# Bias rows on 128 partitions, an earlier end of a graph's preparation, and two neighbour rows scaled on GpSimd, in a graph network kernel

## The chip, the cores and the metric

The kernel runs on one core of a Trainium2 chip. The metric is the device time of the whole program in microseconds: 4361.47 us is the median of three runs before the change (4359.83 to 4365.68). The engines are named as the profile does: PE is TensorE (matmuls), PEld its weight loads, DVE is VectorE, ACT is ScalarE, POOL is GpSimd, SP is SyncE, which here only issues DMAs.

## The reference, cut to what matters

There are 32 graphs of 512 nodes with 128 features. The adjacency is sparse, about one entry in sixteen.

```python
# layer 0
adj  = adj + eye
dis  = adj.sum(axis=2) ** -0.5
x    = layernorm(x + dis[:, :, None] * adj * dis[:, None, :] @ (x @ W) + bias)
# layer 1, over all pairs i, j
m_j, m_i = x @ W1[:D], x @ W1[D:]
pre  = m_j[:, None, :, :] + m_i[:, :, None, :] + b1
msg  = gelu(layernorm(pre, g1, be1))             # exact gelu
agg  = einsum('bijo,bij->bio', msg, adj)
upd  = layernorm(concat([x, agg]) @ W2 + b2, g2, be2)
out  = layernorm(x + upd)
```

Only pairs with an edge count in `agg`, and the kernel works on those alone.

## The kernel before, in words

For each graph and each of its four tiles of 128 destination nodes the kernel lists the neighbours of every node. A slot (a *neighbour row*) takes one neighbour j on each of 128 partitions. A tile has 40 neighbour rows, cut into seven **units** of 6, 6, 6, 6, 6, 5 and 5 rows; a graph has 28 units (GC), the program 896. The rare tile with more neighbours goes through an overflow loop.

The layer norm of a pair is `r * (mj + mi) + be1` after its means are taken out of the weights. Its factor r is found for all pairs of a graph beforehand, as a reciprocal square root. For one unit c the work passes the engines in this order, a step apart each, and every engine runs its own list in order (`steps(cx, i)` is that list for step i):

- DVE in step c-1 makes `pick` (a one-hot matrix with r as its value), L998 and L993.
- PE in step c: two matmuls with a 3-row operand put the bias be1 into PSUM (`z_even_ps` or `z_odd_ps`, L1260), and five or six fp32 matmuls of `mi_g` with `pick` add to it (L1264). The three rows are be1 split into three bf16 parts, multiplied with three rows of ones.
- ACT in step c+1 copies r out of PSUM (L643) and scales the neighbour rows of the unit with it (`tmp`, L647), one instruction for each row.
- DVE in step c+2 adds `tmp` to PSUM (`msg`, L969 and L972) and makes `spread` from the adjacency (L1028, L1024).
- ACT in step c+3 applies the gelu (L634).
- PE in step c+4 adds the unit into `agg_even_ps` or `agg_odd_ps` (L1227).

There are two z buffers, two `tmp` buffers and four `msg` buffers. z of unit c waits for the DVE addition of unit c-2 (`c_z`).

Between these stand three side jobs. **Preparation** of the next graph but one part at a time: step i does part s = (i + 8) mod 28, by the numbers S_XT, S_DEG, ... at the top of the file. PE parts share the bank `p_ps`, in the order of the numbers F_XT, ... : each waits until the one before was copied out. The end of it, in order: h_g (S_H), its transpose (S_HT), miT, mjT (L1123), the norms of mj (S_NRM, L1135), four matmul pairs for the variances (S_V, L1146 and L1147), then on ACT in one part two copies, a table load, the reciprocal square root of 2048 columns (S_SEED, L578), and with the next gelu a second table load; then one correction of the root in four parts (S_ROOT, ACT L583 and L586, DVE L856 and L859), and four parts of four indirect DMAs each on POOL (S_SCATTER, L449), which write all of it by neighbour rank into a table in HBM. SP then reads the table back (`nbr`, `nbr_root`, `nbr_heavy`) when all 16 have landed, in `read`.

**Sorting** of the next tile: from step 3 of each seven, PE transposes `nbr` (T_EDGE, L1159) and `nbr_root` (L1165), and counts edges with triangular matrices (L1169, L1173, and four matmuls onto 32 partitions each, L1178). The first L1159 of a graph waits for the read-back of that graph's table. **Finishing** of the graph before: u (L1241 to L1243, the last of them with 3 rows of b2), statistics, scale, residual and the store.

POOL's list has, beside the scatter, the sums over `pre_g`, the edge mask (L417), powers of -1/2 (L391, L396, L463), the residual (L466, L469), `hb_g` (L432), copies of `mj_g` into `stage` (L425) and `rank_heavy` (L455).

## Time and profile before

| | |
|---|---|
| median of three runs | 4361.47 us |
| profiled execution, its own time | 4369.12 us |
| its span | 4367.4 us |
| mean granted clock | 0.96 of full |
| PE busy | 4004.6 us, 92% |
| ACT busy | 3479.5 us, 80% |
| DVE busy | 3154.2 us, 72% |
| POOL busy | 1499.9 us, 34% |
| first unit's bias matmul starts | 141.5 us |

A busy share is the time in which at least one instruction of the engine ran, by the record. An idle time before an instruction is put down to what came last. Where a row says "issue", the engine's own instruction stream brought the next one only then. The 28 units of a graph take about 129 to 134 us; the stretch from 2150 to 2280 us that is read below is one of them, from unit 0 to unit 27.

### The profile page before, as it was taken

What the parts mean: (1) busy time and instruction counts of PE and PEld (TensorE: products, weight loads), DVE (VectorE), ACT (ScalarE), POOL (GpSimd) and SP (SyncE); (2) the same over time, 40 slices, a digit from 0 to 9 for tenths busy, and PEclk for the clock granted to TensorE, in tenths of its full rate; (3) what the DMA queues carried; (4) which work ended last, traced back from release to release, by engine and by line L of the source; (5) the groups of instructions that cost most, each with busy time, mean ns of one, the idle gap of its engine ahead of it and who ended that gap; (6) DMA issues with size and microseconds to landing.
All of it is one profiled execution on the core that took longest, in us unless ns stands there. A gap on an engine that the chain in (4) does not pass through costs nothing.

```text
span 4367.4 us, 95715 instructions
## 1 busy us (share of the span) xinstructions
PE 4004.6 (92%) x30270; PEld 3283.8 (75%) x30399; DVE 3154.2 (72%) x6981; ACT 3479.5 (80%) x9481; POOL 1499.9 (34%) x1205
## 2 busy tenths in 40 slices
PE   3799999999989999999999999999999999999998
PEld 2677777777768777778777777777777777777776
DVE  3577777777767777767777768777777777768776
ACT  2687888878868878877887878888888888878887
POOL 2333432233413334323343233343233343223331
PEclk8899999999989999999999999999999999999999
DMA  1222221122202222112221112222122221112210
GB/s 42 72 70 78 70 73 38 57 79 78 71 24 64 79 70 78 44 52 72 78 71 65 41 61 78 79 70 68 37 62 79 78 71 62 46 59 78 66 58 15
DMA packets 245645, 276.71 MB, mean 63 GB/s; under 512 B 22320, under 2 KB 204080, under 8 KB 245040
## 3 DMA queue, kind: packets, MB, share of 16 engines
q1 hardware_dynamic: 212272, 168.62, 12.9%
q0 software_dynamic: 32768, 100.70, 6.2%
q8 instruction: 298, 4.88, 0.5%
q14 instruction: 307, 2.51, 0.2%
HBM read 160.17 MB, written 109.05 MB: 62 GB/s over the span
## 4 chain that ended last, share of the span: by engine, by line
PE 56%; ACT 12%; issue 11%; POOL 9%; DVE 5%; DMA 4%; SPq 2%; POOLq 0%; DVEq 0%; ACTq 0%; PEldq 0%
PE z_even_ps L1264 11%; POOL table L449 9%; PE agg_odd_ps L1227 9%; PE z_odd_ps L1264 8%; PE agg_even_ps L1227 7%; ACT tmp L647 4%; PE z_even_ps L1260 3%; PE z_odd_ps L1260 2%; DMA nbr_heavy<-table 2%; PE p_ps L1146 2%; PE p_ps L1147 2%; PE p_ps L1090 2%; DMA table<-stage,row_id 2%; ACT msg L634 2%; ACT root L578 1%
## 5 line engine op out<-in xcount | busy, mean ns | idle before, releaser
L647 ACT ACTIVATE tmp<-nbr,r_sb 128x128 f32<-128x128 f32 x4864 | 1519.3, 389 | 29.1
L998 DVE SCALAR_TENSOR_TENSOR pick<-rank,root_p 128x512 f32<-128x512 bf16 (+3 forms) x1664 | 895.5, 566 | 69.8 <-ACT rank L597 69.8
L1028 DVE SCALAR_TENSOR_TENSOR spread<-rankT,nbr 128x512 f32<-128x512 bf16 (+3 forms) x1664 | 918.7, 580 | 0.0
L449 POOL DMA_INDIRECT table<-stage,row_id x512 | 617.9, 1207 | 551.5 <-issue 504.9
L1264 PEld LDWEIGHTS z_even_ps<-mi_g,pick 128*128 128x128 f32 x5120 | 643.9, 201 | 152.2 <-issue 152.2
L634 ACT ACTIVATE msg<-msg 128x768 f32<-128x768 f32 (+1 forms) x896 | 727.7, 812 | 32.3 <-issue 29.2
L1264 PE MATMUL z_even_ps<-mi_g,pick 128*128 128x129 f32 x5120 | 733.0, 295 | 0.0
L1264 PEld LDWEIGHTS z_odd_ps<-mi_g,pick 128*128 128x128 f32 x5120 | 608.8, 192 | 144.8 <-issue 144.8
L1264 PE MATMUL z_odd_ps<-mi_g,pick 128*128 128x129 f32 x5120 | 694.9, 285 | 0.0
L1227 PE MATMUL agg_odd_ps<-spread,msg 128*128 128x128 f32 x5120 | 671.8, 282 | 21.4 <-DVE spread L1028 19.3
L1227 PEld LDWEIGHTS agg_odd_ps<-spread,msg 128*128 128x128 f32 x5120 | 636.0, 199 | 24.1 <-DVE spread L1028 23.5
L1227 PE MATMUL agg_even_ps<-spread,msg 128*128 128x128 f32 x5120 | 647.2, 276 | 0.0
L1227 PEld LDWEIGHTS agg_even_ps<-spread,msg 128*128 128x128 f32 x5120 | 610.6, 193 | 0.0
L972 DVE TENSOR_TENSOR msg<-z_odd_ps,tmp 128x768 f32<-128x768 f32 x320 | 305.1, 954 | 357.5 <-ACT tmp L647 356.5
L972 DVE TENSOR_TENSOR msg<-z_even_ps,tmp 128x768 f32<-128x768 f32 x320 | 305.1, 954 | 261.2 <-ACT tmp L647 257.8
L455 POOL TENSOR_TENSOR rank_heavy<-rank,behind 128x256 bf16<-128x256 bf16 x128 | 110.8, 865 | 746.2 <-ACT rank L597 745.5
L643 ACT COPY r_sb<-z_even_ps 128x6 f32<-128x6 f32 x448 | 71.1, 159 | 275.0 <-PE z_even_ps L1264 271.6
L425 POOL COPY stage<-mj_g 128x512 f32<-128x512 f32 x128 | 95.1, 784 | 556.0 <-ACT mj_g L557 556.0
L969 DVE TENSOR_TENSOR msg<-z_odd_ps,tmp 128x384 f32<-128x384 f32 (+1 forms) x256 | 112.7, 480 | 222.3 <-ACT tmp L647 220.3
L417 POOL TENSOR_SCALAR edge<-adj_g 128x512 bf16<-128x512 f32 x128 | 263.8, 2078 | 26.3 <-ACT edge L519 26.3
L1260 PE MATMUL z_even_ps<-be_split,ones 3*128 3x387 bf16 x896 | 231.4, 339 | 25.7 <-DVE msg L972 14.6
L1260 PE MATMUL z_odd_ps<-be_split,ones 3*128 3x387 bf16 x896 | 223.6, 329 | 12.1 <-DVE msg L972 1.5
(206 smaller groups left out, 5129.6 us busy)
## 6 DMA issues: line engine op xcount, KB each, us to landing
nbr<-table SPq DMA_DIRECT2D x128, 512.0 KB, 4.0
adj_g<-in_adj SPq DMA_DIRECT2D x32, 1024.0 KB, 5.5
nbr_root<-table SPq DMA_DIRECT2D x128, 256.0 KB, 4.7
nbr_heavy<-table SPq DMA_DIRECT2D x512, 32.0 KB, 3.6
x_g<-in_x SPq DMA_DIRECT2D x32, 256.0 KB, 2.9
table<-stage,row_id POOLq DMA_INDIRECT x512, 2.7
out<-out_sb SPq DMA_DIRECT2D x32, 256.0 KB, 2.3
w_sb<-in_L_gnn_W SPq DMA_DIRECT2D x2, 128.0 KB, 2.3
```

Of the source, the lines that this page charges most:

```text
L417: last = pool.tensor_scalar(edge[:, it, :], adj_g[:, it, :], 0.0, 0.0, ALU.is_equal, ALU.is_equal)
L449: pool.indirect_dma_start(table[q], bass.IndirectOffsetOnAxis(ap=row_id[:, jt * TB + it:jt * TB + it + 1], axis=0), stage[:, jt, it, :], N ...
L455: pool.tensor_tensor(rank_heavy[:, at(k), :, :], rank[:, at(k), 0:HEAVY_W].unsqueeze(1).to_broadcast([P, HEAVY_TILES * HEAVY_T, HEAVY_W]), ...
L634: act.activation(msg[:, c % MSGS, 0:size, :], msg[:, c % MSGS, 0:size, :], ACT.Gelu).then_inc(c_msg, 1)
L647: last = act.activation(tmp[:, c % 2, n - FROM[u], :], half_row, ACT.Identity, scale=r_sb[:, c % 2, n - FROM[u]:n - FROM[u] + 1])
L969: last = dve.tensor_tensor(msg[:, c % MSGS, span, :], z_cols[c % 2][:, h, 0:span.stop - span.start, 0:D], tmp[:, c % 2, span, :], ALU.add)
L972: last = dve.tensor_tensor(msg[:, c % MSGS, :, :].rearrange("p (h k) d -> p h k d", h=2), z_cols[c % 2][:, :, :, 0:D], tmp[:, c % 2, :, :] ...
L998: ins = dve.scalar_tensor_tensor(into.rearrange("p k n -> p (k n)"), rank[:, it, span], float(MARK + t), root_p[:, it, span], ALU.is_equal ...
L1028: ins = dve.scalar_tensor_tensor(into, rankT[:, it, jt:jt + count, :], float(MARK + t), nbr[:, it, jt:jt + count, 0:P], ALU.is_equal, ALU. ...
L1227: last = mm(agg_ps[it % 2][:, 0, 0:P], msg[:, c % MSGS, n - FROM[u], :], spread[:, n % RING, :], start=(n == 0), stop=True, skip_group_che ...
L1260: mm(z[:, h, :, :].rearrange("p k w -> p (k w)"), ones3[:, :], be_split[:, :, :].rearrange("p k w -> p (k w)"), start=True, stop=False, sk ...
L1264: last = mm(z[:, w // 3, w % 3, :], pick[:, n % RING, :], mi_g[:, q, it, :], start=False, stop=True, skip_group_check=True)
```

## The change

The diff has four parts. First, the 3-row operands `b2_split`, `mi_split`, `be_split` and `ones3` become tiles of 128 partitions whose rows 3 to 127 are zero (the ones are `ones_b`), and the four narrow matmuls L1178 become one of 128x128, for which DVE copies the first 32 columns of `edge_p` four times into `edge_heavy`. Second, the parts from S_H to S_OVERS are done one or two steps earlier (S_H 12 to 11, S_V 17..20 to 15..18, S_SEED 21 to 19, S_ROOT 23 to 21, S_SCATTER 24 to 22). Third, for that the norms leave `p_ps`: they go to four free columns of `agg_odd_ps` with semaphores of their own, and `places` and `shift1` are made somewhat earlier on DVE. Fourth, in steps 25, 26, 27, 0 to 9, 12 and 13 of every 28, POOL computes the last two rows of `tmp` and ACT the others; DVE then waits for both.

```diff
+SHARED = tuple(i % GC in (25, 26, 27, 0, 1, 2, 3, 4, 5, 6, 7, 8, 9, 12, 13) for i in range(GC))
+PAIR = 2
...
-S_Y, S_H, S_HT, S_MIT, S_MJT, S_NRM = 9, 12, 13, 14, 15, 16
-S_V = (17, 18, 19, 20)
-S_HB, S_MJ, S_MI, S_SEED, S_ROOT, S_SCATTER, S_OVER, S_OVERS = 18, 21, 22, 21, 23, 24, 23, 27
+S_Y, S_H, S_HT, S_MIT, S_MJT, S_NRM = 9, 11, 12, 13, 14, 15
+S_V = (15, 16, 17, 18)
+S_HB, S_MJ, S_MI, S_SEED, S_ROOT, S_SCATTER, S_OVER, S_OVERS = 18, 19, 20, 19, 21, 22, 21, 26
...
-        be_split = sb("be_split", [3, 3, D + 1], BF16)
-        ones3 = sb("ones3", [3, P], BF16)
+        be_split = sb("be_split", [P, 3, D + 1], BF16)
...
             def steps(cx, i):
+                c = i - 1
+                if cx.known(c) and c < PC and shared(c):
+                    _, it, u = where(c)
+                    n, w = FROM[u + 1] - PAIR, SIZES[u] - PAIR
+                    rows = (nbr_heavy[:, it, P:2 * P].unsqueeze(1).to_broadcast([P, PAIR, D]) if SOURCE[n] == HEAVY
+                            else nbr[:, it, SOURCE[n]:SOURCE[n] + PAIR, P:2 * P])
+                    pool.wait_ge(c_r, cx.units + (c + 1))
+                    pool.tensor_tensor(tmp[:, c % 2, w:w + PAIR, :], rows,
+                                       r_sb[:, c % 2, w:w + PAIR].unsqueeze(2).to_broadcast([P, PAIR, D]), ALU.mult).then_inc(c_pair, 1)
...
-                    for n in range(FROM[u], FROM[u + 1]):
+                    for n in range(FROM[u], FROM[u + 1] - (PAIR if shared(c) else 0)):
...
-                            last = mm(dst, ones3[:, :], mi_split[:, :], start=False, stop=True)
+                            last = mm(dst, ones_b[:, :], mi_split[:, :], start=False, stop=True)
...
-                    for m in range(HEAVY_T):
-                        last = mm(p[m * HEAVY_W:(m + 1) * HEAVY_W, 0:P], edge_p[:, 0:HEAVY_W], lower[:, :], start=True, stop=True)
-                    last.then_inc(t_fill, 1)
+                    pe.wait_ge(t_edge, n + 1)
+                    mm(p[:, 0:P], edge_heavy[:, :, :].rearrange("p k w -> p (k w)"), lower[:, :], start=True, stop=True).then_inc(t_fill, 1)
...
-                        mm(z[:, h, :, :].rearrange("p k w -> p (k w)"), ones3[:, :], be_split[:, :, :].rearrange("p k w -> p (k w)"),
+                        mm(z[:, h, :, :].rearrange("p k w -> p (k w)"), ones_b[:, :], be_split[:, :, :].rearrange("p k w -> p (k w)"),
                            start=True, stop=False, skip_group_check=True)
```

On PE, in the first tile of a graph, the norms and the variance pairs (`p_ps<-miT,mjT`) before the change:

```order
L1227 MATMUL agg_even_ps<-spread,msg 128x128 x6
L1123 MATMUL p_ps<-hT,w_sb 128x512
L1178 MATMUL t_ps<-lower,edge_p 32x128 x4
L1260 MATMUL z_odd_ps<-be_split,ones 128x387 x2
L1264 MATMUL z_odd_ps<-mi_g,pick 128x129 x6
L1227 MATMUL agg_even_ps<-spread,msg 128x128 x6
L1135 MATMUL p_ps<-ones,sqj 128x1 x4
L1260 MATMUL z_even_ps<-be_split,ones 128x387 x2
L1264 MATMUL z_even_ps<-mi_g,pick 128x129 x6
L1227 MATMUL agg_even_ps<-spread,msg 128x128 x5
L1146 MATMUL p_ps<-miT,mjT 128x512
L1147 MATMUL p_ps<-sqi,halves 128x512
```

And in the changed program, the same place:

```order
L1257 MATMUL agg_even_ps<-spread,msg 128x128 x6
L1166 MATMUL agg_odd_ps<-ones,sqj 128x1 x4
L1177 MATMUL p_ps<-miT,mjT 128x512
L1178 MATMUL p_ps<-sqi,halves 128x512
L1209 MATMUL t_ps<-lower,edge_heavy 128x128
L1290 MATMUL z_odd_ps<-be_split,ones_b 128x387 x2
L1294 MATMUL z_odd_ps<-mi_g,pick 128x129 x6
```

The first variance pair stands two units earlier, and norms, pair and the counting matmul share one step.

On ACT, the part with the table loads and the reciprocal square root (`root<-var`) before, beside scaled rows of a five-row unit:

```order
L643 COPY r_sb<-z_even_ps 128x6
L647 ACTIVATE tmp<-nbr,r_sb 128x128 x5
L557 COPY mj_g<-p_ps 128x512
L578 ACT_TABLE_LOAD
L578 ACTIVATE root<-var,eps_col 128x2048
L583 ACTIVATE half<-root 128x512
L600 CAST rankT<-t_ps 128x512
L634 ACT_TABLE_LOAD
L634 ACTIVATE msg<-msg 128x768
```

And in the changed program, with the step that follows:

```order
L671 ACTIVATE tmp<-nbr,r_sb 128x128 x6
L687 COPY u_sb<-agg_even_ps 128x128
L581 COPY mj_g<-p_ps 128x512
L602 ACT_TABLE_LOAD
L602 ACTIVATE root<-var,eps_col 128x2048
L607 ACTIVATE half<-root 128x512
L618 COPY root_p<-t_ps 128x512
L658 ACT_TABLE_LOAD
L658 ACTIVATE msg<-msg 128x768
L667 COPY r_sb<-z_odd_ps 128x6
L671 ACTIVATE tmp<-nbr,r_sb 128x128 x4
L590 COPY mi_g<-p_ps 128x4x128
```

The same block stands two steps earlier, in a step that keeps all six rows on ACT; the step behind it has four.

On POOL, from the scatter to the end of the graph in the changed program (before, the same rows stood in this order without the `tmp` rows):

```order
L464 DMA table<-stage,row_id 2048x384 x16
L470 TENSOR_TENSOR rank_heavy<-rank,behind 128x256
L416 TENSOR_TENSOR pre_g<-x_g,vecs 128x512
L432 TENSOR_SCALAR edge<-adj_g 128x512 x4
L406 TENSOR_TENSOR x_y<-x_v,minus_half 128x8
L494 TENSOR_TENSOR tmp<-nbr,r_sb 128x256 x2
L423 TENSOR_TENSOR half<-sup,dis 128x512
L426 TENSOR_TENSOR pre_g<-pre_g,half 128x512
L494 TENSOR_TENSOR tmp<-nbr,r_sb 128x256
```

The first shared `tmp` of a graph's end is queued behind the sixteen indirect DMAs, the mask and a power.

## Rows read from the trace of the kernel before

**Rows 1.** The page: busy time of each engine, share, instructions.
```profile
PE 4004.6 (92%) x30270; PEld 3283.8 (75%) x30399; DVE 3154.2 (72%) x6981; ACT 3479.5 (80%) x9481; POOL 1499.9 (34%) x1205
```

**Rows 2.** Stretches: length, then busy PE, PEld, DVE, ACT, POOL (instructions), clock, DMA, GB/s.
```profile
2150.00:2193.00 43.00, 42.17 (x343) 33.86 (x340) 33.84 (x77) 36.34 (x106) 8.63 (x6) 1.00 0.08 23
...
2193.00:2246.60 53.60, 51.27 (x387) 41.66 (x389) 39.72 (x88) 48.67 (x125) 21.02 (x21) 1.00 0.14 49
...
2195.10:2206.40 11.30, 11.15 (x70) 7.94 (x70) 5.29 (x14) 8.12 (x22) 0.00 (x0) 1.00 0.01 2
2206.40:2249.60 43.20, 41.02 (x330) 34.63 (x330) 33.44 (x74) 42.32 (x110) 23.69 (x23) 1.00 0.20 72
...
2250.10:2258.30 8.20, 4.86 (x33) 3.77 (x32) 8.20 (x13) 6.08 (x18) 8.20 (x5) 0.89 0.77 217
2258.30:2266.10 7.80, 7.80 (x44) 6.82 (x43) 4.94 (x13) 2.54 (x9) 2.28 (x2) 0.68 0.55 178
```

**Rows 3.** Waits, whole span: who for whom, us in total, times, longest us.
```profile
PEld z_even_ps L1264 <- issue: 152.2, 448, 0.6
PEld z_odd_ps L1264 <- issue: 144.8, 448, 0.6
...
PE t_ps L1159 <- DMA nbr_heavy<-table: 97.7, 28, 9.4
```

**Rows 4.** Timeline of PE, two units: start us, us, engine, line.
```profile
2173.05 1.02 PE L1123 MATMUL p_ps<-hT,w_sb 128*128 128x512 f32 x2
2173.91 0.39 PE L1173 MATMUL t_ps<-lower,edge_p 128*128 128x128 bf16 x4
...
2175.87 1.50 PE L1227 MATMUL agg_even_ps<-spread,msg 128*128 128x128 f32 x12
2177.21 1.02 PE L1123 MATMUL p_ps<-hT,w_sb 128*128 128x512 f32 x2
2178.16 0.24 PE L1178 MATMUL t_ps<-lower,edge_p 128*32 128x128 bf16 x4
...
2187.23 0.50 PE L1260 MATMUL z_odd_ps<-be_split,ones 3*128 3x387 bf16 x2
2187.66 1.61 PE L1264 MATMUL z_odd_ps<-mi_g,pick 128*128 128x129 f32 x12
```

**Rows 5.** Timeline of PE, the 3-row matmuls with mi_split.
```profile
2212.01 0.22 PE L1130 MATMUL p_ps<-mi_split,ones 3*128 3x128 bf16 x1
...
2212.59 0.23 PE L1130 MATMUL p_ps<-mi_split,ones 3*128 3x128 bf16 x1
```

**Rows 6.** Timeline of PE, the DMA wait and the unit behind it.
```profile
2257.26 1.11 PE L1159 MATMUL t_ps<-ident,nbr 128*128 128x128 f32 x4 [3.05 <-DMA nbr_heavy<-table]
...
2259.06 2.95 PE L1264 MATMUL z_even_ps<-mi_g,pick 128*128 128x129 f32 x12
2261.80 2.25 PE L1227 MATMUL agg_odd_ps<-spread,msg 128*128 128x128 f32 x12
```

**Rows 7.** Timeline of POOL: first and last of 16 scatters, the edge mask.
```profile
2224.87 1.37 POOL L449 DMA_INDIRECT table<-stage,row_id  x1 [11.74 <-issue]
...
2247.79 0.96 POOL L449 DMA_INDIRECT table<-stage,row_id  x1 [0.30 <-issue]
...
2250.59 8.33 POOL L417 TENSOR_SCALAR edge<-adj_g 128x512 bf16<-128x512 f32 x4
```

**Rows 8.** Groups by line and shape: count, busy us, mean ns, idle before.
```profile
L647 ACT ACTIVATE tmp<-nbr,r_sb 128x128 f32<-128x128 f32 x4864 | 1519.3, 389 | 29.1
```

**Rows 9.** Timeline of POOL and DVE; last row: durations min/median/max of one line.
```profile
2188.18 1.71 POOL L466 TENSOR_TENSOR res<-res,vecs 128x512 f32<-128x512 f32 x1 [10.64 <-ACT res L613]
...
2188.67 1.76 DVE L1028 SCALAR_TENSOR_TENSOR spread<-rankT,nbr 128x512 f32<-128x512 bf16 x1
...
2240.77 0.65 DVE L1028 SCALAR_TENSOR_TENSOR spread<-rankT,nbr 128x512 f32<-128x512 bf16 x1
...
L411 POOL TENSOR_TENSOR pre_g<-pre_g,half x32: 1267/1273/1279, 55.9 to 4108.6; 128x512 f32<-128x512 f32 x32
```

More of the change, by code:

```diff
@@ L219, in adj_resnorm_kernel @@
         p_scat = [sem(f"p_scat{jt}") for jt in range(TB)]
-        p_seed, p_sq, p_new, p_cube, p_left = (sem(f"p_{n}") for n in ("seed", "sq", "new", "cube", "left"))
+        p_norm, p_normed, p_seed, p_sq, p_new, p_cube, p_left = (sem(f"p_{n}") for n in ("norm", "normed", "seed", "sq", "new", "cube", "left"))
         x_seq, y_seq, z_seq = sem("x_seq"), sem("y_seq"), sem("z_seq")
@@ L223, in adj_resnorm_kernel @@
         t_root = [sem(f"t_root{k}") for k in range(2)]
-        t_fill, t_ev, t_heavy, t_over = (sem(f"t_{n}") for n in ("fill", "ev", "heavy", "over"))
-        (c_pick, c_spread, c_zp, c_r, c_tmp, c_z, c_msg, c_agg) = (
-            sem(f"c_{n}") for n in ("pick", "spread", "zp", "r", "tmp", "z", "msg", "agg"))
+        t_fill, t_ev, t_edge, t_heavy, t_over = (sem(f"t_{n}") for n in ("fill", "ev", "edge", "heavy", "over"))
+        (c_pick, c_spread, c_zp, c_r, c_tmp, c_pair, c_z, c_msg, c_agg) = (
+            sem(f"c_{n}") for n in ("pick", "spread", "zp", "r", "tmp", "pair", "z", "msg", "agg"))
         (e_agg, e_aggc, e_u, e_uc, e_st2, e_shift2, e_upd, e_scaled, e_res, e_st3, e_shift3, e_out, e_store) = (
@@ L723, in _ @@
             step(dve.tensor_tensor(b1_all, b1_all, g1_all, ALU.mult))
[L724 to L726 removed]
+            for rows in (mi_split[:, :], b2_split[:, :], be_split[:, :, :]):
+                step(dve.memset(rows, 0.0))
+            split(mi_split[0:3, :], b1_all)
+            split(b2_split[0:3, :], b2_all)
             for k in range(3):
[L728 to L729 removed]
+                split(be_split[0:3, k, 0:D], be1_all)
             step(dve.memset(x_v[:, :], 1.0))
@@ L962, in steps @@
                     dve.wait_ge(c_tmp, g + (c + 1))
+                    if shared(c):
+                        dve.wait_ge(c_pair, cx.shares + shared_to(c))
                     if cx.known(c - MSGS):
@@ L1129, in prepare @@
                         if s == S_MI:
-                            last = mm(dst, ones3[:, :], mi_split[:, :], start=False, stop=True)
+                            last = mm(dst, ones_b[:, :], mi_split[:, :], start=False, stop=True)
                     last.then_inc(p_fill, 1)
                 if s == S_NRM:
-                    free(F_NRM)
+                    pe.wait_ge(p_ev, a * NF + (F_MJT + 1))
+                    if not is_int(a, 1):
+                        pe.wait_ge(p_normed, a)
                     for jt in range(TB):
-                        last = mm(p[:, jt:jt + 1], sqj[:, jt * P:(jt + 1) * P], ones[:, 0:1], start=True, stop=True)
-                    last.then_inc(p_fill, 1)
+                        last = mm(agg_ps[1][:, 0, NORM + jt:NORM + jt + 1], sqj[:, jt * P:(jt + 1) * P], ones[:, 0:1], start=True, stop=True)
+                    last.then_inc(p_norm, 1)
                 if s == S_OVER:
```

43 lines of the change are left out of this document (24 added, 19 removed).

## The prediction

> **What bounds the kernel now.** I read the busy times first, then the waits, then one graph of 28 units cut into stretches, and last the timeline of PE. PE is busy 92% of the span, ACT 80%, DVE 72% and POOL 34% [rows 1]. These are averages over three kinds of stretch. In units 0 to 9 PE is busy 42.17 of 43.00 us, ACT only 36.34: PE is the bound [rows 2]. From unit 12 on, behind the two table loads and the long root, ACT is busy 42.32 of 43.20 us: there ACT is the bound, PE follows with small gaps [rows 2]. At unit 23 PE stands still for the read-back of the table, 28 times and 97.7 us in all [rows 3]; that stretch of 8.20 us has PE busy 4.86 us, and the next one runs at a granted clock of 0.68 [rows 2]: PE fell from its 2.4 GHz level to 1.2 GHz after standing idle, and twelve passes take 2.95 us instead of 1.61, or 2.25 instead of 1.50 [rows 6, 4]. A busy PE also hides something: 896 times the first weight load of a unit comes 0.33 us late with nothing to wait for, 152.2 + 144.8 us [rows 3].
>
> **Part 1, full rows (PE).** The timeline shows what those 0.33 us are. The two 3-row matmuls take 0.50 us by record and the z matmuls start 0.43 us after them (2187.23, 2187.66) [rows 4]. A bf16 matmul streams 128 columns in 0.057 us (0.39 for the four of L1173 less one record of 0.22, over three) [rows 4, 5], so 387 columns need 0.172, two of them 0.345, and 0.08 is lost. The twelve z passes take 1.61 us where twelve agg passes take 1.50 [rows 4]: 0.10 lost in the first. Going in costs too: behind two 0.43 us passes the full-size bf16 matmul L1173 starts exactly 0.86 us later, but the one on 32 columns, L1178, 0.95 later [rows 4], so 0.09 or 0.10. That is 0.28 us a unit, 896 x 0.28 = 251 us. The 3-row matmul among full ones in L1130 comes round every 0.58 us (2212.01 to 2212.59) [rows 5], where one at 0.06 and two passes of L1128 at 0.11 to 0.125 (1.50 over twelve) [rows 4] make 0.28 to 0.31: say 0.30 x 128 = 38 us. L1243 has the same form, 128 times, some 0.24: 31 us. Four narrow L1178 become one: about 0.1 x 128 = 13 us. Sum 333 us of PE time. Bounds: nothing, if the loss is not one of shape, and 0.36 a unit (0.33 and a bias distance of 0.161), 400 us in all. I take 333, since each piece was read off between neighbours of both kinds.
>
> The Trainium skill (TensorEngine Tiling (Array Packing), Key Properties) says that a change of tiling mode drains TensorE. By that rule the whole loss goes once all operands have one shape; the trace agrees, in that only matmuls of 3 rows or 32 columns have it.
>
> **Part 2, the preparation two units earlier.** What is moved goes along whole: the matmuls on PE, the root and its corrections on ACT and DVE, and 16 indirect DMAs on POOL. The chain to the read-back is long: the first scatter starts at 2224.87, the last at 2247.79, and PE gets its tile at 2257.26, 32.4 us after the first scatter [rows 7, 6]. PE stood idle for it 3.05 us. Two units earlier is about 7 us, but units get shorter by 0.28 each over the ten in between, and the root's block still delays ACT first. That leaves roughly 2 us in hand, so I take the wait as gone: 98 us. Behind it goes the stretch at the lower clock: 1.34 + 0.75 us for the 24 passes [rows 6, 4] and some 0.8 for the rest, 2.9 x 28 = 81, of which I take 75 since some graphs lose less. Sum 173 us; bounds 0 (the wait only moves) and 200. Norms in another bank cost nothing by themselves. `places` and `shift1` can make DVE wait for PE and POOL up to 1 us, in units 0 to 9, where DVE has 9.2 us free of 43 [rows 2].
>
> **Part 3, POOL takes two rows of `tmp` in 15 of 28 units.** ACT is spared 480 x 2 x 0.312 (1519.3 over 4864) = 300 us [rows 8]. POOL gets 480 operations of 256 columns. None stands in the trace; the nearest is L411 with two full operands of 512 columns, 1.27 us [rows 9], half of it 0.64; bounds 0.5 and 1.3. So POOL goes from 1500 to about 1810 us, still far from full. But DVE pays: an operation L1028 beside POOL's L466 took 1.76 us where another took 0.65, 1.11 longer, close to the 1.22 us that L466 still had to run [rows 9]. So an operation of POOL can hold back a pick or spread for its whole length. Per shared unit that is 0 to 0.64 us of DVE; I take 0.45, as about two thirds of DVE's work there is picks and spreads. 480 x 0.45 = 216 us on an engine with 1213 us free, nearly all beside PE; where DVE is tight (units 26 to 1) it costs some 0.5 us a graph, 15 us. The addition can start when ACT has four rows and POOL two; POOL's are done first.
>
> The Trainium skill (SBUF — State Buffer, SBUF: two separate sides) calls this an exclusive lock: whichever starts first has the ports for the whole instruction, against DVE operations with two SBUF operands. The 1.76 us agree with it.
>
> **What ACT and DVE give back.** In units 10 to 22 PE needs 51.27 us today in 53.60 [rows 2]. The change takes 12 x 0.28 = 3.4, two variance pairs that go ahead of it (3.5: each four passes of 0.43), and 2 us of parts 1's small terms: 42.5 are left. ACT's work from r of unit 10 to r of unit 22 is 8.12 + 42.32 = 50.4; two scalings of the variance (1.4) and four rows (1.2) go, 47.8 stay. ACT may fall behind by some 1.5 us more than now. So the twelve units take about 47, and PE idles 4.5 us there instead of 2.3. Unit 23 and 24, where DVE is 100% busy beside the edge mask (8.20 of 8.20, POOL too) [rows 2], add about 2 us that the DMA wait covers today. Together 4.2 x 31 graphs = 130 us.
>
> **The sum.** -333 - 173 + 15 + 130 = -361 us on the profiled execution's 4369 us: 4008. The median of the runs shown is 8 us under that execution, so 4000. The first 141 us (the preparation of graph 0 alone, no units) gain nothing, which the counts allow for. Setup has a few more writes, under 1 us.
>
> **Rivals.**
> 1. *The gap is not one of shape* but of bf16 between fp32. For it: every 3-row matmul is bf16 and stands between fp32 ones. Against: L1173 is bf16, full, and goes in without loss [rows 4]. Then part 1 falls away, ACT and DVE give back only about 50: -173 + 15 + 50, 4250. Chance 5%.
> 2. *The wait stays in part.* The faster units eat the two that were won; PE then idles 1 to 3 us a graph, and the clock falls again. Of 173 about 120 stay: 4120. For it: ready and wanted lie within 2 us. Against: PE's new idle time at ACT's block comes after the move and delays the wish more than the scatter. Chance 17%.
> 3. *ACT gives back less.* If the lag behind PE can grow as far as the buffers let it, PE idles only 2 us more: 4000 - 80 = 3920. Chance 18%.
> 4. *DVE becomes the bound* in the shared units: each POOL operation costs 0.64, twice where it strikes pick and spread. 480 x 0.6 on PE's path is 290 less the 15 counted: 4275 at most, 4120 if half. Chance 10%.
> 5. *Slower.* POOL's list is in order: the first shared `tmp` (unit 24) is queued behind 16 scatters, the mask until 2258.9 [rows 7] and a power. The addition of that unit waits for it, then PE two units on. Today POOL would be free about when ACT starts that unit; the move gives it a few us of lead. It decides if POOL is late by more than 361/31 = 11.6 us a graph, as when the scatters stand 2.5 us apart under DVE's load (15 distances in 22.9 us, 1.5 each, now [rows 7]). Then 4400. Chance 2%.
>
> **Numbers.** My forecast, 4000, has 48%, its own range 3955 to 4060. The range for 8 in 10 takes in rival 3 and most of 2 and 4: 3890 to 4150. About 9 us (0.2%) is what a measurement here can tell from nothing. Faster by more: all but rival 5 and what I did not think of, 0.95; within: 0.02; slower: 0.03.
>
> **What would show it.** Part 1: no "issue" wait before the z weight loads, z start 0.35 us or less behind the bias, twelve z passes in 1.50 us. Part 2: the row PE L1159 on the DMA gone, mean clock above 0.98. Part 3: ACT busy near 3180, POOL near 1810 and its new operation 0.64 us, DVE busy near 3400. Giving back: more PE idle from unit 12 to 24, ended by DVE's addition. I am wrong if the bias matmul itself gets longer with 128 rows, if PE still waits for the table, or if DVE's waits for POOL's `tmp` are more than some tens of us.

## The result, and the profile after

The changed kernel takes 4227.75 us, median of four runs (4223.53 to 4236.44); the kernel before, run beside it, 4363.58. The ratio is 0.969, 95% interval 0.967 to 0.971: 3.1% faster. The forecast was 4000, range 3890 to 4150: right in sign, too good by 5.7%. The profiled execution took 4223.53 us, 145.6 less than before, where the sum said 361.

Busy times, from the page of the changed kernel (answers [rows 1]):

```profile
PE 3708.2 (88%) x30014; PEld 3326.4 (79%) x30015; DVE 3234.7 (77%) x7110; ACT 3217.2 (76%) x8521; POOL 2106.7 (50%) x1685
```

PE has 296 us less to do, yet its share fell from 92 to 88%: it stands still longer than before. Its waits, from the view of waits, whole span (answers [rows 3]):

```profile
PE t_ps L1190 <- DMA nbr_heavy<-table: 183.8, 26, 9.3
...
PEld z_even_ps L1294 <- issue: 5.7, 33, 0.2
...
PEld z_odd_ps L1294 <- issue: 0.5, 3, 0.2
```

The two "issue" waits of 152.2 and 144.8 us are gone. The wait for the read-back, which the move was to end, went from 97.7 to 183.8 us. The timeline of PE, a plain unit and then the wait (answers [rows 4, 6]):

```profile
2077.88 1.50 PE L1294 MATMUL z_even_ps<-mi_g,pick 128*128 128x129 f32 x12
...
2100.42 0.39 PE L1204 MATMUL t_ps<-lower,edge_p 128*128 128x128 bf16 x4
2100.64 0.49 PE L1290 MATMUL z_even_ps<-be_split,ones_b 128*128 128x387 bf16 x2
2100.97 1.28 PE L1294 MATMUL z_even_ps<-mi_g,pick 128*128 128x129 f32 x10
2102.09 1.50 PE L1257 MATMUL agg_even_ps<-spread,msg 128*128 128x128 f32 x12
...
2184.31 1.11 PE L1190 MATMUL t_ps<-ident,nbr 128*128 128x128 f32 x4 [7.17 <-DMA nbr_heavy<-table]
2185.21 0.85 PE L1290 MATMUL z_even_ps<-be_split,ones_b 128*128 128x387 bf16 x2
2185.86 2.50 PE L1294 MATMUL z_even_ps<-mi_g,pick 128*128 128x129 f32 x12
```

z starts 0.33 us behind the bias (2100.64, 2100.97) instead of 0.43, twelve z passes take 1.50 us (2077.88) instead of 1.61, and L1290 starts 0.22 us behind the first of the four L1204, 0.055 for each of them: no loss on the way in. But PE stood 7.17 us at 2184, and behind it twelve passes take 2.50 us: for part of that stretch it was at 1.2 GHz, as before. The same graph in stretches, from the view of windows (columns as in [rows 2]):

```profile
2077.55:2119.20 41.65, 40.97 (x341) 35.26 (x340) 35.97 (x80) 32.18 (x87) 13.59 (x15) 1.00 0.08 24
2119.20:2175.50 56.30, 51.78 (x430) 47.16 (x429) 45.75 (x101) 51.95 (x137) 34.48 (x24) 1.00 0.15 54
2175.50:2184.30 8.80, 1.35 (x11) 0.92 (x9) 3.73 (x6) 4.23 (x12) 8.78 (x6) 0.82 0.53 148
2184.30:2190.50 6.20, 6.19 (x39) 5.95 (x40) 2.73 (x7) 1.70 (x6) 5.49 (x4) 0.71 0.61 181
```

Most of the loss is in the third stretch, 8.80 us with PE busy 1.35; the fourth is granted a clock of 0.71. PE waits there for the read-back. POOL is busy all through it, with work that stands behind the scatter in its list and so came late as well. What ACT and POOL do in the whole span, by line and shape (count, busy us, mean ns, idle before); the last row is the scatter in the kernel before:

```profile
L671 ACT ACTIVATE tmp<-nbr,r_sb 128x128 f32<-128x128 f32 x4032 | 1276.2, 390 | 29.2
L464 POOL DMA_INDIRECT table<-stage,row_id x512 | 881.8, 1722 | 310.5 <-issue 275.5 <-DVE stage L883 20.4 <-DVE x_v L786 7.3
L494 POOL TENSOR_TENSOR tmp<-nbr,r_sb 128x256 f32<-128x256 f32 x416 | 312.5, 751 | 1207.8 <-ACT r_sb L667 1207.6
...
L449 POOL DMA_INDIRECT table<-stage,row_id x512 | 617.9, 1207 | 551.5 <-issue 504.9 <-DVE stage L859 46.3 <-ACT edge L519 0.3
```

The 512 scatters, which no line of the diff touches but for their place, take 881.8 us instead of 617.9, 1.72 us each instead of 1.21. POOL's timeline of that graph (answers [rows 7]):

```profile
2142.63 1.12 POOL L464 DMA_INDIRECT table<-stage,row_id  x1 [4.64 <-issue]
2144.06 3.33 POOL L464 DMA_INDIRECT table<-stage,row_id  x1 [0.30 <-issue]
2147.69 3.91 POOL L464 DMA_INDIRECT table<-stage,row_id  x1 [0.31 <-issue]
2151.90 2.97 POOL L464 DMA_INDIRECT table<-stage,row_id  x1 [0.30 <-issue]
2155.18 0.96 POOL L464 DMA_INDIRECT table<-stage,row_id  x1 [0.30 <-issue]
...
2174.72 1.72 POOL L464 DMA_INDIRECT table<-stage,row_id  x1 [0.30 <-DVE x_v L786]
```

From the first to the last scatter it is 32.1 us, where it was 22.9. From the first scatter to PE's tile it is 41.7 (2142.63 to 2184.31) instead of 32.4. PE wanted the tile at 2177.14. With the old 32.4 it would have been there at 2175.0: the 2 us in hand that the prediction worked out were there, and 9.2 us of longer scatter ate them.

Beside it DVE's timeline, the same stretch. `msg` reads PSUM; `stage` and what is left out behind it read two operands in SBUF:

```profile
2146.47 0.95 DVE L1001 TENSOR_TENSOR msg<-z_even_ps,tmp 128x768 f32<-128x768 f32 x1
2147.34 0.68 DVE L883 SCALAR_TENSOR_TENSOR stage<-half,root 128x512 f32<-128x512 f32 x1
...
2150.68 0.95 DVE L1001 TENSOR_TENSOR msg<-z_odd_ps,tmp 128x768 f32<-128x768 f32 x1
2151.55 0.68 DVE L883 SCALAR_TENSOR_TENSOR stage<-half,root 128x512 f32<-128x512 f32 x1
...
2153.95 0.95 DVE L1001 TENSOR_TENSOR msg<-z_even_ps,tmp 128x768 f32<-128x768 f32 x1
```

The third scatter starts 0.35 us into `stage` (2147.69 less 2147.34), runs beside six DVE operations that read two SBUF operands (`stage` to `spread`), and ends at 2151.60, 0.92 us after the next `msg`, which reads PSUM, began. The next starts 0.30 us later, again 0.35 us into `stage`, and ends 0.92 us after the `msg` at 2153.95. One late end sets up the next.

### The profile page after: what moved, and what is told of

Its sections match the earlier page's. It is cut to its first block, busy times and chain, and to the rows that moved or that the text cites. A ratio compares the mean times of both kernels' runs of the same rounds, so it can differ in the third digit from the quotient of the medians.

```text
span 4221.7 us, 95626 instructions
## 1 busy us (share of the span) xinstructions
PE 3708.2 (88%) x30014; PEld 3326.4 (79%) x30015; DVE 3234.7 (77%) x7110; ACT 3217.2 (76%) x8521; POOL 2106.7 (50%) x1685
## 4 chain that ended last, share of the span: by engine, by line
PE 58%; DVE 15%; ACT 11%; issue 7%; DMA 4%; POOL 2%; SPq 1%; DVEq 1%; ACTq 0%; POOLq 0%; PEldq 0%
PE agg_even_ps L1257 10%; PE z_even_ps L1294 10%; PE z_odd_ps L1294 8%; PE agg_odd_ps L1257 7%; DVE pick L1027 4%; DVE spread L1057 3%; PE p_ps L1177 3%; PE p_ps L1178 3%; PE z_even_ps L1290 3%; ACT tmp L671 2%; PE p_ps L1119 2%; PE z_odd_ps L1290 2%; DMA nbr_heavy<-table 2%; DMA table<-stage,row_id 2%; ACT root L602 2%
## 5 line engine op out<-in xcount | busy, mean ns | idle before, releaser
L671 ACT ACTIVATE tmp<-nbr,r_sb 128x128 f32<-128x128 f32 x4032 | 1276.2, 390 | 29.2
L464 POOL DMA_INDIRECT table<-stage,row_id x512 | 881.8, 1722 | 310.5 <-issue 275.5
L1057 DVE SCALAR_TENSOR_TENSOR spread<-rankT,nbr 128x512 f32<-128x512 bf16 (+3 forms) x1664 | 977.8, 615 | 0.0
L494 POOL TENSOR_TENSOR tmp<-nbr,r_sb 128x256 f32<-128x256 f32 x416 | 312.5, 751 | 1207.8 <-ACT r_sb L667 1207.6
L1294 PE MATMUL z_even_ps<-mi_g,pick 128*128 128x129 f32 x5120 | 675.1, 283 | 0.0
L1294 PE MATMUL z_odd_ps<-mi_g,pick 128*128 128x129 f32 x5120 | 647.9, 276 | 0.0
L1290 PE MATMUL z_even_ps<-be_split,ones_b 128*128 128x387 bf16 x896 | 232.9, 343 | 66.6 <-DVE msg L998 33.3
L1190 PE MATMUL t_ps<-ident,nbr 128*128 128x128 f32 x512 | 94.5, 315 | 197.2 <-DMA nbr_heavy<-table 183.8
L1190 PEld LDWEIGHTS t_ps<-ident,nbr 128*128 128x128 f32 x512 | 65.9, 160 | 225.6 <-DMA nbr_heavy<-table 177.7
L1290 PE MATMUL z_odd_ps<-be_split,ones_b 128*128 128x387 bf16 x896 | 222.1, 330 | 10.6 <-DVE msg L1001 9.6
```

Source lines behind the costliest of these rows:

```text
L464: pool.indirect_dma_start(table[q], bass.IndirectOffsetOnAxis(ap=row_id[:, jt * TB + it:jt * TB + it + 1], axis=0), stage[:, jt, it, :], N ...
L494: pool.tensor_tensor(tmp[:, c % 2, w:w + PAIR, :], rows, r_sb[:, c % 2, w:w + PAIR].unsqueeze(2).to_broadcast([P, PAIR, D]), ALU.mult).the ...
L671: last = act.activation(tmp[:, c % 2, n - FROM[u], :], half_row, ACT.Identity, scale=r_sb[:, c % 2, n - FROM[u]:n - FROM[u] + 1])
L1057: ins = dve.scalar_tensor_tensor(into, rankT[:, it, jt:jt + count, :], float(MARK + t), nbr[:, it, jt:jt + count, 0:P], ALU.is_equal, ALU. ...
L1190: last = transpose(p[:, jt * P:(jt + 1) * P], nbr[:, at(k), jt, 0:P], ident[:, :])
L1290: mm(z[:, h, :, :].rearrange("p k w -> p (k w)"), ones_b[:, :], be_split[:, :, :].rearrange("p k w -> p (k w)"), start=True, stop=False, s ...
```

## The experiments

All ratios are to the kernel before on the same chip, with a 95% interval. "Scatter" is the start of the 16th scatter less that of the first in POOL's timeline, median of graphs 2 to 32; "wait" the row of PE's first transpose on the DMA, whole span. Times marked * are from a chip on which the kernel before took 4575 or 4573 us; on the others it took 4362 to 4368. "Full rows" is the first part of the diff, "move" the second and third, "shared" the fourth; "by tile" is a read-back of a tile that waits for the scatters into that tile alone.

| kernel | us | ratio | scatter | wait |
|---|---|---|---|---|
| before | 4361 | 1 | 22.9 | 97.7 |
| changed | 4228 | 0.969 [0.967, 0.971] | 32.1 | 183.8 |
| full rows alone | 4170 | 0.956 [0.953, 0.958] | 23.2 | 137.8 |
| full rows, move | 4082 | 0.936 [0.933, 0.939] | 25.9 | 56.7 |
| move alone | 4226 | 0.968 [0.965, 0.971] | 24.5 | 11.5 |
| full rows, shared | 4166 | 0.955 [0.952, 0.957] | 23.2 | 127.2 |
| changed again | 4238 | 0.970 [0.968, 0.972] | 32.1 | 193.9 |
| 18 memsets between | 4003 | 0.916 [0.915, 0.918] | 23.4 | 11.0 |
| 18 memsets at msg | 4029 | 0.924 [0.922, 0.926] | 26.0 | 19.0 |
| memsets, no shared | 4003 | 0.918 [0.917, 0.920] | 23.5 | 10.4 |
| no shared, by tile | 4012 | 0.919 [0.917, 0.920] | 25.9 | 10.4 |
| 13 shared units | 4059 | 0.932 [0.929, 0.935] | 25.9 | 41.3 |
| memsets, by tile | 3996 | 0.916 [0.915, 0.918] | 23.4 | 6.4 |

### The parts one by one

The full rows alone (part 1 of the diff, put into the kernel before):

```diff
-        be_split = sb("be_split", [3, 3, D + 1], BF16)
-        ones3 = sb("ones3", [3, P], BF16)
...
+        be_split = sb("be_split", [P, 3, D + 1], BF16)
...
```

> The kernel before with the full-row bias operands and the single counting matmul alone; preparation and POOL as before. Theory P: the 16 scatters of a graph stretch (22.9 us before, 32.1 us in the changed kernel, first start to last start) because of where they stand against DVE's operations with two SBUF operands, that is because of the move. Then the scatter stays at 23 us here, the wait of the first L1159 grows only by what PE is faster in the units between, from 3.1 to about 5 us a graph, and the time is about 4200 us. Rival Q: it stretches because PE, and with it DVE, runs faster. Then the scatter takes 28 us or more here, the wait is 8 us or more, and the time about 4290 us.

Measured 4169.87 us: 192 us less. PE's busy time fell by 309 (4005 to 3696), but the wait for the read-back grew by 40: the units are shorter, the scatter is not.

The changed kernel without shared units, so full rows and move:

```diff
-SHARED = tuple(i % GC in (25, 26, 27, 0, 1, 2, 3, 4, 5, 6, 7, 8, 9, 12, 13) for i in range(GC))
+SHARED = tuple(i % GC in () for i in range(GC))
```

> The changed kernel with all rows of tmp on ACT. P: scatter still about 32 us and a wait of about 7 us a graph; ACT busy 3480 us again, some units of 0 to 9 become bound by ACT, 4240 to 4280 us. Rival R: it is POOL's new operations that delay the scatter (a late start, or the ports): then the scatter returns to 23 us, the wait nearly vanishes, and the time is under 4130 us.

Measured 4082.08: 146 us faster than the changed kernel. At the new places sharing costs that. It isn't DVE's or POOL's load in the shared units 0 to 9: from the bias of unit 0 to that of unit 12 both kernels take 53.2 us (median of graphs 3 to 30). From unit 23 to unit 24, across the read-back, they take 11.9 with sharing and 6.8 without.

The move alone (three-row operands back, no shared units):

```diff
-SHARED = tuple(i % GC in (25, 26, 27, 0, 1, 2, 3, 4, 5, 6, 7, 8, 9, 12, 13) for i in range(GC))
+SHARED = tuple(i % GC in () for i in range(GC))
...
-        be_split = sb("be_split", [P, 3, D + 1], BF16)
+        be_split = sb("be_split", [3, 3, D + 1], BF16)
+        ones3 = sb("ones3", [3, P], BF16)
...
```

> The changed kernel with 3-row operands, the four narrow matmuls, and all rows of tmp on ACT: what is left is the end of preparation two units earlier and the norms in another bank. P: scatter about 32 us although PE is no faster, the two units (7 us) are spent on that, the wait stays at 3 to 6 us, time 4350 to 4400 us. Q or R: scatter 23 us, the wait is gone, 4200 us or less.

Measured 4225.65, 137 us less, wait 11.5. Here the move does what it was priced for, nearly: the forecast for it was 173.

The changed kernel with the places of before (full rows and shared units):

```diff
-S_V = (15, 16, 17, 18)
-S_HB, S_MJ, S_MI, S_SEED, S_ROOT, S_SCATTER, S_OVER, S_OVERS = 18, 19, 20, 19, 21, 22, 21, 26
...
+S_V = (17, 18, 19, 20)
+S_HB, S_MJ, S_MI, S_SEED, S_ROOT, S_SCATTER, S_OVER, S_OVERS = 18, 21, 22, 21, 23, 24, 23, 27
```

> The changed kernel with the numbers S_H to S_OVERS as before (full rows and shared tmp stay, and so does the bank of the norms). P: scatter 23 us, wait about 5 us a graph instead of 7.3; the time is then at or below the changed kernel's 4228, about 4180 us. Q or R: scatter 30 us or more, and since it starts two units later the wait is 12 us or more, 4350 us or more.

Measured 4165.73 beside 4169.87 without sharing: at the old places it is worth nothing and costs nothing. So the loss takes the move and the sharing together (with full rows; the two without them were not run), and it sits in the length of the scatter. None of the three theories named ahead of these runs holds in all four: P (the move alone) fails where the move alone has a scatter of 24.5 us, Q (a faster PE) where the full rows alone have 23.2, and R (POOL's new operations) at the old places, with 23.2.

### Which shared units, and a read-back that waits for less

The scatters signal by the tile that they fill:

```diff
-                                            stage[:, jt, it, :], None).then_inc(p_scat[jt], 16)
+                                            stage[:, jt, it, :], None).then_inc(p_scat[it], 16)
...
```

> The changed kernel, and the sixteen scatters signal by the destination tile that they fill instead of by the source tile. The read-back of tile 0 then waits for the four scatters of tile 0, of which the last is the 13th of sixteen, and no longer for the 16th. If PE's wait (7.3 us a graph, 26 graphs) and the cold clock behind it are set by the end of the scatter, as I think: the last three scatters are 5 to 6 us of the 32.1, so the wait falls to some 2 us a graph (about 50 us in all), the time in half-clock stretches from 343 to about 150 us, and the time to about 4120 us (4080 to 4160). The length of the scatter itself stays 32 us. Rival (the wait only moves to the transfers or to the mask that share the queue and POOL): above 4190, with a wait of over 5 us a graph left.

4356.35* us, ratio 0.952 [0.950, 0.953]: the wait gone (6.8 us), the scatter as long as before the edit (32.0), and the time above its neighbours on that chip below. The edit brought a wait of its own: ACT's refill of `stage` for the next graph now waits for all sixteen. From the view of waits of this kernel:

```profile
ACT stage L550 <- DMA table<-stage,row_id: 357.0, 28, 16.1
```

Only units 12 and 13 out of the shared ones, and only they in:

```diff
-SHARED = tuple(i % GC in (25, 26, 27, 0, 1, 2, 3, 4, 5, 6, 7, 8, 9, 12, 13) for i in range(GC))
+SHARED = tuple(i % GC in (25, 26, 27, 0, 1, 2, 3, 4, 5, 6, 7, 8, 9) for i in range(GC))
```

> The changed kernel, but units 12 and 13 keep all six rows of tmp on ACT (13 shared units of 28 instead of 15). Units 12 and 13 are the last shared ones ahead of the scatter. If it is their effect on where DVE and POOL stand when the scatter starts that makes it 32 us instead of 26: the scatter comes back to about 26 us, PE's wait to 2 or 3 us a graph, and the time to about 4085 us (4070 to 4110), as with no shared unit at all (4082). Rival (the shared units 25 to 27 and 0 to 9 cost it, by what POOL's operations hold back on DVE): about 4190 to 4230 with a scatter of over 29 us.

```diff
+SHARED = tuple(i % GC in (12, 13) for i in range(GC))
```

> The changed kernel with only units 12 and 13 shared (2 of 28 instead of 15). The mirror of the kernel before it. If units 12 and 13 are the cause, the loss is all here: a scatter near 32 us, PE's wait 6 to 7 us a graph, 4200 to 4235 us. Rival (the other thirteen shared units): scatter near 26 us and about 4085 us. If both this kernel and the one before it are near 4085, it takes both kinds of units together.

4141.12* and 4247.47*, ratios 0.906 [0.902, 0.910] and 0.929 [0.927, 0.930], scatters of 22.8 and 32.1 us. The two units just ahead of the scatter carry the loss, the thirteen others don't. On a chip like the first the former ran again:

> The kernel that keeps all rows of tmp of units 12 and 13 on ACT, once more, beside kernels on a chip like the first (if this is one). Expected: a scatter near 23 to 26 us, PE's wait under 60 us in all, no waits by 'remote', and 4075 to 4090 us as without any shared unit (4082). Rival (the other thirteen shared units do harm too): 4130 us or more.

4059.32 us, scatter 25.9: as without any sharing or a little better (4075 to 4090 were expected).

### Memsets on DVE

A memset of 128x16, which reads nothing, ahead of every pick and spread in steps 14 to 18 (18 a graph, where my expectation said about 15):

```diff
+                        if i % GC in (14, 15, 16, 17, 18):
+                            dve.memset(door[:, doors[0] % 15, :], 0.0)
+                            doors[0] += 1
```

> The changed kernel with one more DVE operation, a memset of 128x16 that reads nothing, ahead of every pick and every spread in steps 14 to 18, about 15 a graph, some 0.06 us each (1 us of DVE a graph). In the traces a scatter that starts beside DVE operations with two SBUF operands lasts until shortly after DVE's next operation with a PSUM operand. If it is such a run of operations that holds POOL's descriptor writing, a gap at each operation lets POOL in: the scatters shorten from 2.0 to about 1.5 us, all sixteen from 32 to 25 or 27 us, and the time falls to 4080 to 4130 us in spite of the added work. Rival (POOL is held for another reason, or a memset is no gap, since POOL has to wait for the operation that is in flight anyway): 31 us or more and 4225 to 4260 us.

4319.09* us. The scatter was shorter than expected (20.4 us instead of 25 to 27), the time longer. Since the kernel before was slow on that chip too, I ran before, changed and this one on one chip, with a by-tile version without shared units that has a semaphore for each scatter (there ACT's `stage` waits 13.0 us for the scatters, not 357.0):

> The kernel before, unchanged, for a trace from the same chip as the three beside it. In the last job the kernel before took 4575 us, where the two jobs ahead of it had 4362 to 4364. There the kernels with a scatter of 23 us or less (the doors, and the one without units 12 and 13) had waits in their traces whose end nothing profiled explains (PE's first transpose 105 us by 'remote' and 150 us by 'issue', ACT's r_sb 279 us by 'remote'), and those with a scatter of 32 us had few. If a fast scatter meets a chip that feeds instructions or semaphores more slowly: on such a chip this trace shows such waits for some 200 us and 4575 us; on a chip like the first two, none and 4362 us. Rival (that chip's clock or HBM is slower all over): the extra time is spread over all steps.

> The changed kernel, unchanged, as the measure for the two beside it on one chip. Expected 4228 us with a scatter of 32 us, on either kind of chip, since its scatter is slow on both; then its ratio to the kernel before is 0.969 on a chip like the first and 0.924 on one like the last. Rival (the chips differ in everything): 4430 us on a chip of the last kind.

> The kernel with a DVE memset ahead of each pick and spread in steps 14 to 18 once more, now beside the changed kernel on one chip. Its scatter took 20.4 us, 1.06 us for each of the sixteen, as the theory of the port wants, but steps 16 to 18 of a graph took 22.0 us instead of 11.5. If those 10 us belong to the chip: on a chip like the first two its steps 16 to 18 take 12 us and it runs in 4040 to 4100 us. Rival (the memsets or the denser transfers cost it anywhere): 4300 us or more here too.

```diff
-        p_scat = [sem(f"p_scat{jt}") for jt in range(TB)]
+        p_scat = [[sem(f"p_scat{jt}{it}") for it in range(TB)] for jt in range(TB)]
...
```

> The changed kernel with no shared unit, and with a semaphore for each of the sixteen scatters: the read-back of a tile waits for its own four scatters, while the refill of stage waits for just those that read it. My first version by tile signalled by destination alone, and ACT's refill of stage then waited for the end of the scatter (357 us): that was a fault of my edit, not an answer. Without shared units PE waited 16 times, 57 us, and 202 us ran at half clock. The last scatter ahead of tile 0's read becomes the 13th: about 4 us earlier. I expect no wait left, 150 us or less at half clock, and 4020 to 4050 us on a chip like the first two, ratio 0.923 to 0.929. Rival (the wait is already of no weight, other things hold PE at that place): 4075 to 4085 us.

4368.56, 4237.69, 4002.56 and 4012.34 us. This chip behaves like the first two. 576 more DVE operations make the changed kernel 235 us faster, and the kernel then takes what the forecast said (4040 to 4100 were expected of it). The by-tile version came out below its expectation of 4020 to 4050; against the kernel without sharing its scatter is the same 25.9 us and its wait 10.4 instead of 56.7, so it is the end of the scatter that PE waits for. The busy times with the memsets, from the page of that kernel:

```profile
PE 3643.4 (91%) x29886; PEld 3279.3 (82%) x30015; DVE 3276.6 (82%) x7686; ACT 3220.6 (80%) x8521; POOL 1882.1 (47%) x1685
```

I had taken the memset for a gap through which POOL gets at SBUF. The control puts the same memsets behind `msg`, where they break no run:

```diff
                     last.then_inc(c_z, 1)
+                    for m in range({14: 4, 15: 4, 16: 4, 17: 3, 18: 3}.get(i % GC, 0)):
+                        dve.memset(door[:, 4 * (i % GC - 14) + m if i % GC < 17 else 12 + 3 * (i % GC - 17) + m, :], 0.0)
```

> The changed kernel with the same number of DVE memsets a graph (18, of 128x16) in the same steps 14 to 18, but all behind the addition that makes msg, which has a PSUM operand and lets a scatter through anyway. So the work and the time added are the same and no run of operations with two SBUF operands is broken. Port theory: the scatters stay long, sixteen of them take 29 us or more, PE's wait stays over 4 us a graph, and the time is 4170 to 4250 us. Rival (phase: any 0.3 us more on DVE moves the scatters to better places): about 23 us and 4000 to 4050 us, like the memsets ahead of picks and spreads (4003).

4029.09 us, scatter 26.0. The expectation of the gaps fails; the rival (any small shift on DVE is enough) has the time right, with a scatter 3 us longer than it said. Two more, beside it:

> The kernel without shared units and with the memsets ahead of picks and spreads. Port theory: a scatter of 23 us or less instead of 25.9, PE's wait (57 us over 16 graphs) gone, 4005 to 4020 us, much like the one that signals by tile (4012) and some us behind the shared one with the same memsets (4003). Rival (the gaps helped only because of POOL's new operations): scatter stays 26 us and 4080 us.

> The changed kernel with both remedies, the memsets ahead of picks and spreads and a semaphore for each scatter. With the memsets alone two waits of 11.7 us and 156 us of half clock were left at 4003 us; so signalling by tile has little left to win: 3990 to 4003 us. Rival (ACT and DVE, not the wait, hold PE behind unit 22, and a read-back that starts earlier takes DMA time from the scatter): same or up to 4020 us.

4002.69 and 3996.45 us, both about as expected. The last has the lowest time, but its ratio is that of the memsets alone: signalling by tile adds nothing to them.

### Where a scatter starts

Why does a shift help? The timeline of the kernel without shared units, graph 21 from its third scatter on:

```profile
2582.90 0.96 DVE L1001 TENSOR_TENSOR msg<-z_even_ps,tmp 128x768 f32<-128x768 f32 x1 [0.22 <-ACT tmp L671]
...
2583.77 0.68 DVE L883 SCALAR_TENSOR_TENSOR stage<-half,root 128x512 f32<-128x512 f32 x1
2583.82 1.47 POOL L464 DMA_INDIRECT table<-stage,row_id  x1 [0.30 <-issue]
...
2585.60 1.24 POOL L464 DMA_INDIRECT table<-stage,row_id  x1 [0.31 <-issue]
```

The third scatter starts 5.05 us after the first (2578.77), as in the changed kernel (2147.69 less 2142.63 is 5.06). But DVE's `msg` waits 0.22 us for ACT, which scales all six rows, so `stage` starts 0.3 us later against it, and the scatter starts 0.05 into it instead of 0.35 and takes 1.47 us instead of 3.91. With POOL's help `msg` is 0.3 us earlier, and this scatter takes 2.4 us more, the next 1.7. Fourteen of 31 graphs have their third scatter in `stage` like this one; in fourteen more the second is short already and the third starts in `spread`.

I then sorted all scatters of graphs 2 to 32 in all twenty traces (sixteen different kernels) by the DVE operation (memsets left out) whose record covers their start; for operations of 0.6 us and more with two SBUF operands, by how far into it:

| DVE at the start | scatters | over 2.5 us | median us |
|---|---|---|---|
| idle | 1286 | 0 | 0.96 |
| `msg` | 1907 | 4 | 0.96 |
| two operands, 0 to 0.10 us in | 756 | 183 | 1.48 |
| 0.10 to 0.20 | 192 | 2 | 1.36 |
| 0.20 to 0.32 | 560 | 0 | 1.25 |
| 0.32 to 0.39 | 986 | 713 | 3.03 |
| 0.39 to 0.46 | 969 | 28 | 1.11 |
| 0.46 to 0.52 | 104 | 1 | 1.05 |
| 0.52 to 0.64 | 316 | 0 | 0.96 |

The kernels are much alike, so these are not independent cases. And the offset alone does not decide. The 183 long ones of the first row start 0.06 to 0.09 us into `half`, most of them as second of their graph; in the kernel without shared units 26 second scatters start there, and 12 take 3.3 us, 14 take 1.4. With the memsets at `msg` the eighth scatter starts 0.34 to 0.35 us into `stage` in 26 graphs, beside the same operations as the fourth of the changed kernel, and takes 1.16 us instead of 2.97. So an offset near 0.35 goes with most of the long ones, and what else it takes is open. Two last kernels were to move the offset of the third scatter. A POOL memset ahead of it:

```diff
+                    if n == 2:
+                        pool.memset(pause[:, :], 0.0)
```

> The changed kernel with one more POOL operation a graph: a memset of 128x128, 0.20 us in the trace's setup, ahead of the third of the sixteen scatters. In the changed kernel that scatter starts 0.36 us into DVE's stage operation and takes 3.91 us, and the next starts again at 0.36 and takes 2.97. Offset theory: it now starts at about 0.6, takes 1.0 us, the fourth lands elsewhere too, the sixteen take 25 to 28 us, PE's wait is 60 us or less, and the time 4030 to 4090 us, though POOL was given work and delayed. Rival (the offset only goes along with the load): 32 us and 4230 to 4245 us.

4250.40* us, scatter 32.1. From POOL's timeline of this kernel, with `stage` of DVE:

```profile
2159.12 0.68 DVE L886 SCALAR_TENSOR_TENSOR stage<-half,root 128x512 f32<-128x512 f32 x1
2159.17 0.22 POOL L466 MEMSET pause<- 128x128 f32 x1
2159.56 3.83 POOL L467 DMA_INDIRECT table<-stage,row_id  x1 [0.17 <-issue]
```

The memset hides in most of the 0.30 us between two scatters: the start moved by 0.09 us, to 0.44, not to 0.6, and the scatter ends when it did before. The expectation missed, and the test of a late start wasn't made. The 28 long ones in the row of 0.39 to 0.46 are these; none of the other 941 of that row is over 1.8 us.

A DVE memset of 128x256 behind the addition of step 15 alone:

```diff
+                    if i % GC == 15:
+                        dve.memset(pause[:, :], 0.0)
```

> The changed kernel with one more DVE operation a graph: a memset of 128x256 behind the addition of step 15, so DVE's stage operation, under which the third scatter starts, comes 0.1 to 0.3 us later. Offset theory: the scatter starts at 0.06 to 0.26 instead of 0.36 us into it and takes 1.0 to 1.6 us instead of 3.91; sixteen take 25 to 28 us; 4030 to 4090 us. Rival (it takes eighteen memsets, by their sum or by the gaps they make): 32 us and 4230 us or more.

The start of a graph, from the timeline:

```profile
2974.19 0.62 DVE L884 SCALAR_TENSOR_TENSOR stage<-half,root 128x512 f32<-128x512 f32 x1
2974.58 1.06 POOL L465 DMA_INDIRECT table<-stage,row_id  x1 [0.30 <-issue]
...
2975.94 0.96 POOL L465 DMA_INDIRECT table<-stage,row_id  x1 [0.30 <-issue]
2977.21 0.97 POOL L465 DMA_INDIRECT table<-stage,row_id  x1 [0.31 <-issue]
...
2978.13 0.68 DVE L884 SCALAR_TENSOR_TENSOR stage<-half,root 128x512 f32<-128x512 f32 x1
...
2978.48 1.16 POOL L465 DMA_INDIRECT table<-stage,row_id  x1 [0.30 <-issue]
```

One memset of 0.27 us: scatters of over 2.5 us fall from 147 (changed again) to 16, and the sixteen take 20.4 us instead of 32.1. That is not the chip: on this one the kernels with a long scatter have 32.0 or 32.1 as well, though the short ones are 3 us shorter here (20.4 and 23.4 with the memsets between, 22.8 and 25.9 with 13 shared units). The memset came a step earlier than I thought, under the second scatter, and moved the second and the third; it took effect all the same. The last two rows are the plainest case against the offset as the whole cause: the fifth scatter starts 0.35 us into the same `stage` operation as the third of the changed kernel, with the same six operations on DVE at the same distances, and takes 1.16 us instead of 3.91 (27 of 31 graphs). As to the time the expectation missed: 4313.08*, for on this chip PE and ACT then wait for something that the profile doesn't show:

```profile
PE t_ps L1193 <- remote: 235.6, 27, 12.5
...
ACT r_sb L668 <- remote: 222.5, 45, 6.2
```

On this chip other kernels have such rows too, ACT's of 105 us with the POOL memset and a long scatter, 279 with the memsets between; on the others none is above 5 us. The same file, the memsets between, took 4319 here and 4003 there. What releases them is open.

## Why the prediction was wrong

**Part 1 held.** 0.28 us a unit were forecast; bias to z, first pass and the way in now lose nothing, and PE's work falls by 309 us (full rows alone) where 333 were forecast. Rival 1 is out. (The piece from L1130 comes to 0.27 to 0.30 by its own rows, not 0.28 to 0.31; the 0.30 that was used is its upper end.)

**Part 2 is the step that failed**, by its sentence that the chain is 32.4 us from the first scatter and the wait therefore gone. "Roughly 2 us in hand" was right. The chain is not a constant: 41.7 us in the changed kernel, since sixteen scatters stretch with how they fall against DVE's work. With full rows the move took them from 23.2 to 25.9 us, and the two shared units just ahead of them, 12 and 13, to 32.1: that effect of part 3 on part 2 has no term in the sum. So +86 us of wait in place of -98, and the 75 of the clock were not won: the mean granted clock is 0.96 as before, where 0.98 was forecast. It is the mechanism of rival 5 (scatters further apart "under DVE's load": 2.1 us against 1.5, where it named 2.5), which I had tied to the first shared `tmp` and a price of 11.6 us, not to the read-back, where it decides from 2 us on. I had seen that POOL holds up DVE [rows 9] and not asked for the reverse.

The Trainium skill (SBUF — State Buffer, SBUF: two separate sides) gives that reverse: a DVE operation in a two-port mode holds the shared ports for its whole length, and GpSimd can't write the descriptors of its DMAs meanwhile. The traces agree in so far as a scatter takes 0.96 us beside an idle DVE and up to 3.9 beside its operations. Whether these operations ran in such a mode no run shows. A wait for one operation of 0.68 us is too short for the 3 us that are added, and a start 0.20 to 0.32 us into one costs just 0.3. A lock that each of the operations in a row took anew would reach to the `msg`, as the long ones do; but then the fifth scatter above, with the same row beside it, would be long too. The measurement decides: a lock by whole operations doesn't tell when a scatter is long, and the mechanism stays open.

**Part 3.** POOL's operation is 0.61 us alone, 0.75 in the mean (0.64 forecast), ACT is at 3217 (3180), POOL at 2107 (1810, 264 of the difference are scatters). DVE has 3235, not 3400: 60 more than without sharing, where I took 216. What sharing gives in time is nothing that these runs can tell: 4170 and 4166 at the old places, 4003 and 4003 with memsets. ACT was no bound in the shared units, as [rows 2] said for units 0 to 9; the 300 us spared there were never on the path.

**Given back.** With the scatter short (memsets between) the sum can be read term by term against the trace of before: PE's busy time -361 (forecast -333 - 75), the wait -87 (-98), PE's other idle time +85 (130 + 15). Spans: 4367.4 less 4003.9 is 363.5, and 361 were forecast. The terms partly make up for each other, each is within 61 us, so that the total agrees to 3 us is in part luck. In the changed kernel itself they are -296, +86 and +65, together the 145.7 us of its span.

**Rivals.** Rival 2 had the right place (the wait stays, the clock falls again) but a reason that wasn't it, and ended at 4120. Rival 3's price was 80 where its own 2 us a graph in place of 4.2 make 68, and half of rival 4 comes to 4130 at least, not 4120; neither touches the outcome. The range was no wider because I gave the length of the scatter no bounds.

## What to carry to other kernels

A chain that ends in a DMA from GpSimd has a length that depends on what VectorE runs beside it; before moving such a chain, read the spread of its single pieces, not its sum, and keep that spread as a bound. It stood in the trace of before: in 27 of 31 graphs the eleventh scatter took 3.03 us where most took about 1, and the sixteen of one graph took 48.7. When work is moved off an engine that isn't the bound, as with the rows of `tmp`, what changes may be only how the others fall against each other, and that has a price too. And look at a loss by undoing parts in pairs: full rows alone, the move alone, and sharing with full rows at the old places each kept the scatter under 25 us.
